# Cross-attention over 16 heads: the heads' outputs moved to their rows by GpSimd, straight through SBUF, instead of by SyncE through DRAM

## The chip, the cores and the metric

One of the cores of a Trainium2 chip runs the program. The metric is device microseconds of one execution of the whole program, median of several executions.

## The reference

Two blocks follow each other on x, 8 batches of 100 rows of 512 values; ctx has 361 rows for each batch. All is float32.

```python
# first block: twice cross-attention with 16 heads of 128, then an MLP of 2048
x = x + cross_attention(layer_norm(x), ctx)      # two layers
x = x + gelu(layer_norm(x) @ w_fc1 + b) @ w_fc2 + b
# second block: cross-attention with 16 heads of 32
x1 = layer_norm(x, ln1_w, ln1_b)
q, k, v = x1 @ q_w + q_b, ctx @ k_w + k_b, ctx @ v_w + v_b      # split into 16 heads of 32
attn = softmax(where(mask, q @ k.T / sqrt(32), min))
out = concat_heads(attn @ v) @ cproj_w + cproj_b
x = x + out
x = x + gelu(layer_norm(x) @ fc_w + fc_b) @ proj_w + proj_b
```

The change touches only what lies between `attn @ v` and `@ cproj_w` in the second block.

## The kernel before

Everything is stored turned: features on the 128 partitions, rows of x on the free axis, in two halves of four batches (`ROWS` = 400 columns). A product in float32 is made of three matmuls of parts: each factor is a high part rounded to the matmul's type and a low part, the rest. ScalarE (ACT) writes the high part, VectorE (DVE) the low one, and GpSimd (POOL) splits weights. The order of every engine is written out by hand, and engines meet only at semaphores. Each engine takes its instructions strictly in order.

**The attention of the second block** is a loop of steps `s`, one for each batch `b` = s // 4 and group of four heads `j` = s % 4 (`NS` = 32 steps, and two more to drain). A step has four units, one head each: turn the probabilities of the unit three back (`turn1`), the scores (`logits1`), a part of the keys of step s + 3 (`keys1`), a third of the weighted sums of values of step s - 2 (`value_sums1`). ACT and DVE do the softmax in between.

**The heads' outputs.** `value_sums1(t)` leaves in a PSUM bank, for group t, a 128 x 400 product whose 128 rows are the features of four heads and whose 400 columns are four probability sets. Only the four diagonal blocks of 32 x 100 are wanted. ACT writes the whole product's high part to `heads_out` (`value_sum1_high`, which the profile shows as a write to qs by line 1234), DVE its low part (`value_sum1_low`, qs by line 1495; it raises `y_lo`). In program order both stand in the fourth unit of step t + 2. There is one buffer `heads_out` alone (`qs[1]`). PE may begin `value_sums1(t + 1)` in the first unit of the next step only when `y_lo` says that the low part of t is written, since both use one PSUM bank.

From `heads_out` the blocks go to `attnT` (the profile's qT), where `project1` reads them: at step 19 (`S_CPROJ`) for the first four batches, after the loop for the rest. A block stays on its 32 partitions and only changes columns. SyncE (SP) does it in two transfers by way of DRAM: `save_heads(t)` writes all of `heads_out` (400 KB) to `y_parts`, line 626; `load_heads(t)` waits for that landing, for `c_mm` if the batch is of the second half (`attnT` is free again only when the first `project1` has read it), and reads the four blocks back, line 636. ACT may write `heads_out` for t when save t - 1 has landed:

```python
            act.wait_ge(S.y_out, 16 * s)
```

**SP's queue** begins all transfers of the program. In step s it stands like this: save heads s - 3, `load_k(s + 1)` (keys of the next step back from DRAM, `k<-k_parts`, line 621), `save_k(s + 2)`, context, mask and queries when due, load heads s - 3, then weights (`load_jobs`, line 558). A weight tile goes to one of three staging buffers, and the load waits until POOL has split the tile three before it (`w_ready`).

**POOL's queue** is a list of weight tiles with due times, `JOBS`, in whose gaps the list `extra` puts other work by due times of its own: the loop step counts from `T_ATT1` = 304. In the loop it splits the tiles of `cproj_w` (in_1c, due at steps 14 and 30) and of the MLP (due at step 20), splits the context of batches 2 to 7 (`second_context`, lines 779 and 781, once in four steps), converts masks, and does parts of layer norms 7 and 8 (`norm_sum`, `norm_square_sum`, `norm_scale`, lines 792 to 813). An extra runs as soon as POOL comes to it and its semaphores allow; the due time sets its place only.

Of the kernel before, what the change touches and what calls it, by code (L numbers as in the profile page):

```python
# [12 lines left out]
F32 = mybir.dt.float32  # L13
# [3 lines left out]
P = 128  # L17
BATCH, LQ, LK, D = 8, 100, 361, 512
NB = BATCH // 2
ROWS = NB * LQ  # L20
LT = LK + 1
DC = D // P
# [4 lines left out]
HG = 4  # L27
HD1 = 32
# [14 lines left out]
NS = 2 * 16  # L43
# [74 lines left out]
T_ATT1 = 304  # L118
# [91 lines left out]
def build(nc, T, out):  # L210
# [5 lines left out]
           ("L1_xattn_fc_b", "L1_xattn_proj_b", ACT.Gelu_apprx_tanh)]  # L216

    k_dram = nc.dram_tensor("k_parts", [NS, P, 2, LT], F32, kind="Internal").ap()
    y_dram = nc.dram_tensor("y_parts", [NS, P, 2, ROWS], F32, kind="Internal").ap()
    q_dram = nc.dram_tensor("q_parts", [BATCH, P, 2, 4, LQ], F32, kind="Internal").ap()  # L220

    with ExitStack() as ctx:
# [60 lines left out]
        attnT, heads_out = qT, qs[1]  # L283
# [13 lines left out]
        def sem(name):  # L297
            return ctx.enter_context(nc.semaphore(name))
# [77 lines left out]
        S.y_hi = sem("y_hi")  # L376
        S.y_lo = sem("y_lo")
        S.at_in = sem("at_in")
        S.y_out = sem("y_out")
        S.k1_out = [sem(f"k1_out{k}") for k in range(2)]  # L380
        S.k3_in = [sem(f"k3_in{k}") for k in range(2)]
        S.k1w_in = sem("k1w_in")
# [23 lines left out]
        def f32(ap):  # L406
            return ap.bitcast(F32)
# [115 lines left out]
        AHEAD, BEHIND = 3, 2  # L523
# [27 lines left out]
        def _(sp):  # L551
# [57 lines left out]
            def save_k(s):  # L609
                sp.wait_ge(S.k1_lo, s + 1)  # L610
                sp.dma_start(k_dram[s], f32(kT[:, s % 2])).then_inc(S.k1_out[s % 2], 16)

            def load_k(s):

                sp.wait_ge(S.k1_out[s % 2], 16 * (s // 2 + 1))
                if s >= 2:
                    sp.wait_ge(S.s1_mm, HG * (s - 2) + HG)
                else:
                    sp.wait_ge(S.o_mm, DC * GN)
                for k, _, k_part in PARTS3:  # L620
                    sp.dma_start(f32(k3[k * HD1:(k + 1) * HD1, s % 2]),
                                 k_dram[s, :, k_part].rearrange("(i r) n -> r i n", i=HG)).then_inc(S.k3_in[s % 2], 16)

            def save_heads(t):
                sp.wait_ge(S.y_lo, t + 1)
                sp.dma_start(y_dram[t], f32(heads_out[:])).then_inc(S.y_out, 16)

            def load_heads(t):

                b, j = divmod(t, 4)  # L630
                sp.wait_ge(S.y_out, 16 * (t + 1))
                if b >= NB:
                    sp.wait_ge(S.c_mm, DC)
                for i in range(HG):
                    r, a = slice(i * HD1, (i + 1) * HD1), j * ROWS + b % NB * LQ
                    sp.dma_start(f32(attnT[r, :, a:a + LQ]), y_dram[t, r, :, i * LQ:(i + 1) * LQ]).then_inc(S.at_in, 16)  # L636

            def load_values_weight():
                sp.wait_ge(S.v_tmp, HG * GN)
                sp.wait_ge(S.up_mm, 3)  # L640
                sp.wait_ge(S.dn_mm, 1)
                for j in range(4):
                    sp.dma_start(w1_raw[:, j, 1, :], T["1v"][j]).then_inc(S.v1w_in, 16)
# [54 lines left out]
            save_k(1)  # L698
            load_k(0)
            for s in range(NS + BEHIND):  # L700
                if s >= BEHIND + 1:
                    save_heads(s - BEHIND - 1)
                if s + 1 < NS:
                    load_k(s + 1)
                if s + AHEAD - 1 < NS:
                    save_k(s + AHEAD - 1)
                if s % 4 == 1 and s // 4 + 2 < BATCH:
                    load_ctxT(4 * GN + s // 4 + 2)
                if s % 4 == 2 and s // 4 + 2 < BATCH:
                    load_mask(s // 4 + 2)  # L710
                if s - 1 - S_Q1 in range(4):
                    save_q(4 + s - 1 - S_Q1)
                if s % 4 == 3 and s // 4 + 1 in range(2, BATCH):
                    load_q(s // 4 + 1)
                if s >= BEHIND + 1:
                    load_heads(s - BEHIND - 1)
                load_jobs(jobs_due(T_ATT1 + s - 1) + STAGE)
            save_heads(NS - 1)
            load_heads(NS - 1)
            for F in range(NF):  # L720
                load_jobs(jobs_due(T_MLP[1] + F - 1) + STAGE)
                if F - FF in range(DC):
# [10 lines left out]
        def _(pool):  # L733
# [73 lines left out]
            def norm_scale(li):  # L807
                k = norm_buffer(li)
                pool.wait_ge(S.ln_rstd, 2 * li + 2)
                for c in range(DC):  # L810
                    y = ln_c[k][:, c, :]
                    pool.wait_ge(S.ln_cs, DC * BY_POOL.index(li) + c + 1)
                    nc.gpsimd.tensor_tensor(y, y, lnb[:, 1, :], ALU.mult).then_inc(S.ln_y, 1)  # L813

            extra = [(due, 3, convert_mask, b) for b, due in enumerate(MASK_DUE)]
            extra += [(T_ATT1 + 4 * (b - 2) + 2.2, 2, second_context, b) for b in range(2, BATCH)]
            for n0, li in LN_GROUP.items():
# [2 lines left out]
            extra += [(s7 + 0.3, 0, norm_sum, 7), (s7 + 2.9, 0, norm_square_sum, 7), (s7 + 6.6, 0, norm_scale, 7),  # L820
                      (s8 + 0.95, 0, norm_sum, 8),
                      (s8 + 4.6, 0, norm_square_sum, 8), (s8 + 8.6, 0, norm_scale, 8)]
            extra.sort(key=lambda e: e[:2])
            done = 0
            for j in range(len(JOBS)):
# [406 lines left out]
        def _(act):  # L1232
# [115 lines left out]
            def value_sum1_high(s):  # L1348
                act.wait_ge(S.a_mm, s + 1)
                if s:  # L1350
                    act.wait_ge(S.y_out, 16 * s)
                else:
                    act.wait_ge(S.qs_out[1], 64)
                high(heads_out[:, 0, :], bank[A1_BANK][:, 0:ROWS], col_c("L1_xattn_v_b", s % 4)).then_inc(S.y_hi, 1)
# [563 lines left out]
```

## Time and profile before

| | us |
|---|---|
| median of three runs | 2254.26 |
| the runs | 2253.84, 2254.26, 2258.37 |
| profiled execution | 2260.57 |
| its span, first to last instruction | 2258.8 |
| PE busy | 2161.1 (96%) |
| DVE busy | 1605.4 (71%) |
| ACT busy | 1183.9 (52%) |
| POOL busy | 943.8 (42%) |
| loop of the second block, about | 1790 to 2105 |

The profiled execution is 6.3 us longer than the median of the others. The views are: the windows (busy time of each engine in a stretch), the timeline of an engine (start, duration, instruction, and in brackets how long the engine was idle before and what ended that), the view of one tile, and the chain of what ended last. Times in the timelines count from the start of the span.

### The profile page before, as it was taken

To read this page: it belongs to the slowest core of one execution; us is meant where nothing else is said; L and a number is where in the kernel's file an instruction comes from. 1 tells how busy PE (TensorE), PEld (TensorE's weight loads), DVE (VectorE), ACT (ScalarE), POOL (GpSimd) and SP (SyncE) were. 2 spreads that over 40 slices of the span, in tenths; PEclk is the share of its full clock that TensorE was granted. 3 is DMA by queue.
4 is the path that set the end of the run, shared out by engine and by line. 5 is a ranking of instruction groups with operands and counts; after the bars stand their busy time and mean duration, and the time that the engine had idled before them with its cause. 6 is when DMAs were issued, how large, how long until landed. Compare 5 with 4: busy or idle time off the path is not lost.

```text
span 2258.8 us, 36858 instructions
## 1 busy us (share of the span) xinstructions
PE 2161.1 (96%) x12468; PEld 2099.6 (93%) x12468; DVE 1605.4 (71%) x3635; ACT 1183.9 (52%) x2838; POOL 943.8 (42%) x898
## 2 busy tenths in 40 slices
PE   6999999999999999999999999999999899998899
PEld 5999999999999999999999999998899778887899
DVE  6777688777778877777887777777466487788353
ACT  4555465555555555555555555565243376667232
POOL 4314444241444424234342424432788332232597
PEclk9999999999999999999999999999999999998999
DMA  4646455554645555464555546454543667765243
GB/s 136 140 87 142 102 121 101 120 128 83 151 101 113 102 125 122 85 148 105 110 110 116 126 83 151 109 102 83 139 125 103 167 189 199 206 199 160 84 132 108
DMA packets 162454, 283.08 MB, mean 125 GB/s; under 512 B 35424, under 2 KB 92896, under 8 KB 162272
## 3 DMA queue, kind: packets, MB, share of 16 engines
q1 hardware_dynamic: 162272, 280.73, 52.5%
q8 instruction: 105, 1.72, 0.3%
q14 instruction: 77, 0.63, 0.1%
HBM read 237.66 MB, written 29.88 MB: 118 GB/s over the span
## 4 chain that ended last, share of the span: by engine, by line
PE 80%; DVE 6%; DMA 4%; ACT 3%; POOL 3%; issue 2%; SPq 2%; POOLq 0%; DVEq 0%; ACTq 0%
PE bank L838 76%; PE bank L926 3%; POOL mring L759 1%; DMA ctxN_raw<-in_ctx 1%; POOL mring L757 1%; DVE ln_c L1548 1%; DVE hT L1495 1%; SPq L636 1%; DVE lnb L1541 1%; PE bank L1106 1%; ACT prob L1340 1%; DMA k<-k_parts 1%; DVE prob L1662 1%; POOL ln_c L813 1%; DMA y_parts<-qs 0%
## 5 line engine op out<-in xcount | busy, mean ns | idle before, releaser
L838 PE MATMUL bank<-ctxT,kring 128*128 128x362 f32 x3456 | 629.6, 330 | 4.4 <-DVE qs L1495 2.7
L757 POOL TENSOR_SCALAR mring<-stage 128x512 fp32r<-128x512 f32 x325 | 233.3, 718 | 899.2 <-PE bank L838 734.2
L838 PEld LDWEIGHTS bank<-ctxT,kring 128*128 128x128 f32 x3456 | 587.2, 190 | 7.6 <-issue 4.7
L838 PE MATMUL bank<-pT,ctxN 128*128 128x400 f32 (+1 forms) x2304 | 470.0, 351 | 0.6 <-DVE U L1499 0.3
L759 POOL TENSOR_TENSOR mring<-stage,mring 128x512 fp32r<-128x512 f32 x325 | 444.9, 1369 | 27.1
L838 PEld LDWEIGHTS bank<-pT,ctxN 128*128 128x128 f32 (+1 forms) x2304 | 407.1, 188 | 2.4 <-issue 1.2
L838 PE MATMUL bank<-hT,mring 128*128 128x400 f32 x1608 | 320.0, 348 | 13.8 <-DVE hT L1495 10.5
L838 PEld LDWEIGHTS bank<-hT,mring 128*128 128x128 f32 x1608 | 296.1, 190 | 18.3 <-issue 15.0
L838 PE MATMUL bank<-U,mring 128*128 128x400 f32 x1536 | 303.3, 348 | 8.1 <-issue 6.3
L838 PEld LDWEIGHTS bank<-U,mring 128*128 128x128 f32 x1536 | 275.3, 188 | 10.3 <-issue 7.9
L1234 ACT ACTIVATE kT<-bank,cols 128x361 fp32r<-128x361 f32 (+1 forms) x288 | 160.8, 558 | 211.8 <-PE bank L838 211.7
L1499 DVE TENSOR_TENSOR ctxN<-ctxN_raw,ctxN 128x384 fp32r<-128x384 f32 x256 | 189.2, 742 | 81.9 <-ACT ctxN L1234 81.9
L1234 ACT ACTIVATE U<-bank 128x400 fp32r<-128x400 f32 x256 | 127.8, 499 | 146.2 <-PE bank L838 144.3
L1499 DVE TENSOR_TENSOR U<-bank,U 128x400 fp32r<-128x400 f32 x256 | 146.2, 571 | 74.8 <-ACT U L1234 73.8
L1577 DVE TENSOR_SCALAR_CACHE_REDUCE prob<-bank 100x362 f32<-100x362 f32 x256 | 135.1, 528 | 88.1 <-PE bank L838 88.0
L1282 ACT ACTIVATE prob<-prob,stat 100x362 f32<-100x362 f32 x256 | 151.1, 590 | 74.7 <-DVE prob L1577 74.7
L1234 ACT ACTIVATE pT<-bank 128x300 fp32r<-128x300 f32 x384 | 160.0, 417 | 54.0 <-PE bank L926 37.6
L1499 DVE TENSOR_TENSOR pT<-bank,pT 128x300 fp32r<-128x300 f32 x384 | 175.6, 457 | 5.8 <-ACT pT L1234 5.8
L1234 ACT ACTIVATE ctxN<-ctxN_raw 128x384 fp32r<-128x384 f32 x256 | 131.7, 516 | 85.3 <-DMA ctxN_raw<-in_ctx 85.2
L838 PE MATMUL bank<-kT,qT 128*100 128x362 f32 x768 | 169.2, 328 | 4.2 <-DVE kT L1495 4.2
L1499 DVE TENSOR_TENSOR part<-gtmp,part 128x400 fp32r<-128x400 f32 x64 | 75.3, 1178 | 136.6 <-ACT part L1234 136.3
L1495 DVE SCALAR_TENSOR_TENSOR kT<-bank,cols,kT 128x361 fp32r<-128x361 f32 (+1 forms) x288 | 168.2, 584 | 4.6 <-ACT kT L1234 4.6
(103 smaller groups left out, 2942.1 us busy)
## 6 DMA issues: line engine op xcount, KB each, us to landing
ctxT_raw<-in_ctx SPq DMA_DIRECT2D x72, 724.0 KB, 7.5
ctxN_raw<-in_ctx SPq DMA_DIRECT2D x256, 192.0 KB, 3.6
k<-k_parts SPq DMA_DIRECT2D x96, 181.0 KB, 3.7
stage<-in_wk SPq DMA_DIRECT2D x64, 256.0 KB, 4.1
stage<-in_wq SPq DMA_DIRECT2D x64, 256.0 KB, 4.5
stage<-in_wv SPq DMA_DIRECT2D x64, 256.0 KB, 4.0
stage<-in_wo SPq DMA_DIRECT2D x64, 256.0 KB, 2.7
stage<-in_fa SPq DMA_DIRECT2D x64, 256.0 KB, 2.6
```

The costliest lines, as they stand in the source:

```text
L636: sp.dma_start(f32(attnT[r, :, a:a + LQ]), y_dram[t, r, :, i * LQ:(i + 1) * LQ]).then_inc(S.at_in, 16)
L757: nc.gpsimd.tensor_scalar(hi, src, 1.0, 1.0, ALU.mult, ALU.mult).then_inc(S.w_hi, 1)
L759: nc.gpsimd.tensor_tensor(lo, src, f32(hi), ALU.subtract).then_inc(S.w_ready, 1)
L813: nc.gpsimd.tensor_tensor(y, y, lnb[:, 1, :], ALU.mult).then_inc(S.ln_y, 1)
L838: mm = pe.matmul(dst, parts_l[a], parts_r[b], start=first and k == 0, stop=last and k == len(order) - 1)
L926: mm = pe.transpose(bank[T_BANK][:, t * LQ:(t + 1) * LQ], prob[0:LQ, n % PB, t * P:(t + 1) * P], ident[0:LQ, 0:LQ])
L1106: mm = pe.transpose(bank[T1_BANK[u % 2]][:, t * LQ:(t + 1) * LQ], prob1[0:LQ, u % PB, t * P:(t + 1) * P], ident[0:LQ, 0:LQ])
L1234: return nc.scalar.activation(dst, src, ACT.Identity, bias=bias)
L1282: nc.scalar.activation(x, x, ACT.Exp, scale=-1.0, bias=nmax[0:LQ, k:k + 1], accum_out=denom[0:LQ, k:k + 1]).then_inc(S.exp_ready, 1)
L1495: return nc.vector.scalar_tensor_tensor(out=dst, in0=src, scalar=bias, in1=f32(hi), op0=ALU.add, op1=ALU.subtract)
L1499: return nc.vector.tensor_tensor(dst, src, f32(hi), ALU.subtract)
L1577: nc.vector.tensor_scalar(prob[0:LQ, k, 0:LT], bank[2 + n % 2][0:LQ, 0:LT], -SCALE0, None, ALU.mult, ALU.min, accum_out=nmax[0:LQ, k:k + 1 ...
```

## The change

`save_heads` and `load_heads` leave SP's queue, and with them the DRAM tensor `y_parts` and the semaphore `y_out`. `move_heads(t)` on POOL waits for `y_lo` (and for `c_mm` from t = 16 on) and begins four transfers, each from one block of `heads_out` to its columns of `attnT`. ACT's write of `heads_out` for t now waits until all four transfers of t - 1 have landed (`at_in`). Each `move_heads(t)` is an extra with due time step t + 2.8. The number of matmuls and of ACT, DVE and POOL compute instructions stays as it was.

```diff
-            def save_heads(t):
-                sp.wait_ge(S.y_lo, t + 1)
-                sp.dma_start(y_dram[t], f32(heads_out[:])).then_inc(S.y_out, 16)
-
-            def load_heads(t):
-
-                b, j = divmod(t, 4)
-                sp.wait_ge(S.y_out, 16 * (t + 1))
-                if b >= NB:
-                    sp.wait_ge(S.c_mm, DC)
-                for i in range(HG):
-                    r, a = slice(i * HD1, (i + 1) * HD1), j * ROWS + b % NB * LQ
-                    sp.dma_start(f32(attnT[r, :, a:a + LQ]), y_dram[t, r, :, i * LQ:(i + 1) * LQ]).then_inc(S.at_in, 16)
...
             for s in range(NS + BEHIND):
-                if s >= BEHIND + 1:
-                    save_heads(s - BEHIND - 1)
...
-                if s >= BEHIND + 1:
-                    load_heads(s - BEHIND - 1)
                 load_jobs(jobs_due(T_ATT1 + s - 1) + STAGE)
-            save_heads(NS - 1)
-            load_heads(NS - 1)
...
+            def move_heads(t):
+
+                b, j = divmod(t, 4)
+                pool.wait_ge(S.y_lo, t + 1)
+                if b >= NB:
+                    pool.wait_ge(S.c_mm, DC)
+                for i in range(HG):
+                    r, a = slice(i * HD1, (i + 1) * HD1), j * ROWS + b % NB * LQ
+                    nc.gpsimd.dma_start(f32(attnT[r, :, a:a + LQ]), f32(heads_out[r, :, i * LQ:(i + 1) * LQ]))\
+                        .then_inc(S.at_in, 16)
+
...
+            extra += [(T_ATT1 + BEHIND + t + 0.8, 1, move_heads, t) for t in range(NS)]
...
-                    act.wait_ge(S.y_out, 16 * s)
+                    act.wait_ge(S.at_in, 64 * s)
```

POOL's queue around steps 13 to 15, before. The splits of the four tiles of in_1c (lines 757 and 759, into mring) are followed by the context split (779, 781):

```order
L757 TENSOR_SCALAR mring<-stage 128x512 [waits q1_mm,w_in1]
L759 TENSOR_TENSOR mring<-stage,mring 128x512 [waits w_hi]
L757 TENSOR_SCALAR mring<-stage 128x512 [waits q1_mm,w_in2]
L759 TENSOR_TENSOR mring<-stage,mring 128x512 [waits w_hi]
L757 TENSOR_SCALAR mring<-stage 128x512 [waits q1_mm,w_in0]
L759 TENSOR_TENSOR mring<-stage,mring 128x512 [waits w_hi]
L779 TENSOR_SCALAR ctxT<-ctxT_raw 128x724 [waits ctxT_in1]
L781 TENSOR_TENSOR ctxT<-ctxT_raw,ctxT 128x724 [waits cT_hi]
```

The same place now (lines 735, 737, 757, 759, 801 are the split of a tile, the split of the context and the move):

```order
L801 DMA qT<-qs_92 32x2x100 [waits y_lo]
L801 DMA qT<-qs_92 32x2x100 x3
L735 TENSOR_SCALAR mring<-stage 128x512 [waits q1_mm,w_in0]
L737 TENSOR_TENSOR mring<-stage,mring 128x512 [waits w_hi]
L735 TENSOR_SCALAR mring<-stage 128x512 [waits q1_mm,w_in1]
L737 TENSOR_TENSOR mring<-stage,mring 128x512 [waits w_hi]
L735 TENSOR_SCALAR mring<-stage 128x512 [waits q1_mm,w_in2]
L737 TENSOR_TENSOR mring<-stage,mring 128x512 [waits w_hi]
L735 TENSOR_SCALAR mring<-stage 128x512 [waits q1_mm,w_in0]
L737 TENSOR_TENSOR mring<-stage,mring 128x512 [waits w_hi]
L757 TENSOR_SCALAR ctxT<-ctxT_raw 128x724 [waits ctxT_in1]
L759 TENSOR_TENSOR ctxT<-ctxT_raw,ctxT 128x724 [waits cT_hi]
```

Move 11 has come ahead of the four splits, and move 12 (two rows further on) stands behind them and behind the context split.

SP's queue at step 19, before:

```order
L605 DMA q_86<-q_parts 32x4x400 [waits s1_mm,qs_out1,qs_out0]
L605 DMA q_86<-q_parts 32x4x400 x2
L636 DMA qT<-y_parts 32x2x100 [waits c_mm,y_out]
L636 DMA qT<-y_parts 32x2x100 x3
L626 DMA y_parts<-qs_92 128x800 [waits y_lo]
L621 DMA k_87<-k_parts 32x4x362 [waits s1_mm,k1_out1]
```

SP's queue at step 19 now:

```order
L603 DMA q_86<-q_parts 32x4x400 [waits s1_mm,qs_out1,qs_out0]
L603 DMA q_86<-q_parts 32x4x400 x2
L619 DMA k_87<-k_parts 32x4x362 [waits s1_mm,k1_out1]
L619 DMA k_87<-k_parts 32x4x362 x2
L609 DMA k_parts<-kT 128x724 [waits k1_lo]
```

The wait for `c_mm` has gone from SP. It stands now on POOL, ahead of a layer norm's sum (line 770) and the splits of the MLP's tiles:

```order
L801 DMA qT<-qs_92 32x2x100 [waits c_mm,y_lo]
L801 DMA qT<-qs_92 32x2x100 x3
L801 DMA qT<-qs_92 32x2x100 [waits c_mm,y_lo]
L801 DMA qT<-qs_92 32x2x100 x3
L770 TENSOR_TENSOR lnb<-xT 128x400 [waits qs_out0,c_add]
L773 TENSOR_TENSOR lnb<-lnb,xT 128x400 [waits ln_sum] x2
L735 TENSOR_SCALAR mring<-stage 128x512 [waits c_mm,w_in1]
```

These are moves 16 and 17; four tile splits follow, and then move 18.

## Rows read from the trace of the kernel before

**Rows 1.** Windows: stretch, length, busy us of PE, PEld, DVE, ACT, POOL; PE clock, DMA share, GB/s.

```profile
1945.90:1949.50 3.60, 3.58 (x15) 3.46 (x16) 2.09 (x6) 1.46 (x4) 0.00 (x0) 0.62 0.83 243
```

**Rows 2.** Timeline of PE: its three longest waits for a transfer in the loop.

```profile
1945.92 0.41 PE L1095 MATMUL bank<-k,q 96*100 96x362 f32 x1 [2.85 <-DMA k<-k_parts]
...
2007.80 0.41 PE L1095 MATMUL bank<-k,q 96*100 96x362 f32 x1 [4.50 <-DMA k<-k_parts]
...
2105.46 11.36 PE L838 MATMUL bank<-qT,w 128*128 128x400 f32 x48 [6.59 <-DMA qT<-y_parts]
```

**Rows 3.** Tile y_parts: issue ns (min/median/max) on SP, and issue to landing.

```profile
L636 SPq DMA_DIRECT2D qT<-y_parts x128: 538/594/974, 1815.4 to 2103.2; - x128
...
DMA to landing us min/median/max: 2.0/3.0/5.3
```

**Rows 4.** One size on two engines: POOL's timeline, and the chain's line for DVE.

```profile
1815.20 1.05 POOL L801 TENSOR_TENSOR lnb<-ln_q 128x400 f32<-128x400 f32 x1 [3.19 <-ACT ln_q L1240]
```

```profile
1813.51 0.57 DVE ln_c L1525
```

**Rows 5.** Timeline of ACT and DVE: the heads of t = 31 written, high and low.

```profile
2096.34 0.60 ACT L1234 ACTIVATE qs<-bank,cols 128x400 fp32r<-128x400 f32 x1 [2.04 <-DMA y_parts<-qs]
```

```profile
2096.97 0.63 DVE L1495 SCALAR_TENSOR_TENSOR qs<-bank,cols,qs 128x400 fp32r<-128x400 f32 x1 [2.06 <-ACT qs L1234]
```

**Rows 6.** Timelines of POOL and PE at steps 7 and 8.

```profile
1851.54 4.29 POOL L813 TENSOR_TENSOR ln_c<-ln_c,lnb 128x400 f32<-128x400 f32 x4 [7.13 <-DVE lnb L1541]
```

```profile
1859.64 0.70 PE L838 MATMUL bank<-pT,v 128*128 128x400 f32 x3
```

**Rows 7.** Timelines of SP, POOL and PE at steps 15 and 16.

```profile
1929.75 2.47 SPq L636 DMA_DIRECT2D qT<-y_parts  x4
1932.27 0.58 SPq L558 DMA_DIRECT2D stage<-in_1c  x1
```

```profile
1936.85 0.62 POOL L757 TENSOR_SCALAR mring<-stage 128x512 fp32r<-128x512 f32 x1 [24.94 <-DMA stage<-in_1c]
...
1938.81 0.90 POOL L779 TENSOR_SCALAR ctxT<-ctxT_raw 128x724 fp32r<-128x724 f32 x1
...
1942.39 1.72 POOL L781 TENSOR_TENSOR ctxT<-ctxT_raw,ctxT 128x724 fp32r<-128x724 f32 x1
```

```profile
1935.96 0.70 PE L838 MATMUL bank<-pT,v 128*128 128x400 f32 x3
```

**Rows 8.** Timelines of SP, POOL and PE at steps 19 to 22.

```profile
1980.16 2.46 SPq L636 DMA_DIRECT2D qT<-y_parts  x4
```

```profile
1981.96 2.18 POOL L795 TENSOR_TENSOR lnb<-lnb,xT 128x400 f32<-128x400 f32 x2
```

```profile
1981.35 0.70 PE L838 MATMUL bank<-pT,v 128*128 128x400 f32 x3
...
1996.06 0.71 PE L838 MATMUL bank<-pT,v 128*128 128x400 f32 x3
```

**Rows 9.** Timelines of POOL and PE at steps 24 to 29.

```profile
2019.23 2.24 POOL L805 TENSOR_TENSOR lnb<-lnb,ln_q 128x400 f32<-128x400 f32 x2 [8.81 <-ACT ln_q L1240]
...
2055.09 4.30 POOL L813 TENSOR_TENSOR ln_c<-ln_c,lnb 128x400 f32<-128x400 f32 x4 [32.57 <-DVE lnb L1541]
```

```profile
2026.86 0.70 PE L838 MATMUL bank<-pT,v 128*128 128x400 f32 x3
...
2062.35 0.71 PE L838 MATMUL bank<-pT,v 128*128 128x400 f32 x3
```

**Rows 10.** Timelines of DVE and ACT: heads of t = 27 written, t = 28 begun.

```profile
2069.04 0.63 DVE L1495 SCALAR_TENSOR_TENSOR qs<-bank,cols,qs 128x400 fp32r<-128x400 f32 x1 [0.83 <-ACT qs L1234]
```

```profile
2075.91 0.57 ACT L1234 ACTIVATE qs<-bank,cols 128x400 fp32r<-128x400 f32 x1
```

**Rows 11.** Timeline of DVE: one multiplication, without and with POOL at work.

```profile
1925.71 0.41 DVE L1676 TENSOR_SCALAR prob<-prob,stat 100x361 f32<-100x361 f32 x1
...
1989.49 1.05 DVE L1676 TENSOR_SCALAR prob<-prob,stat 100x361 f32<-100x361 f32 x1
```

More of the change, by code:

```diff
@@ L218, in build @@
     k_dram = nc.dram_tensor("k_parts", [NS, P, 2, LT], F32, kind="Internal").ap()
-    y_dram = nc.dram_tensor("y_parts", [NS, P, 2, ROWS], F32, kind="Internal").ap()
     q_dram = nc.dram_tensor("q_parts", [BATCH, P, 2, 4, LQ], F32, kind="Internal").ap()
@@ L378, in build @@
         S.at_in = sem("at_in")
-        S.y_out = sem("y_out")
         S.k1_out = [sem(f"k1_out{k}") for k in range(2)]
```

## The prediction

> **What bounds the kernel now.** I read four views, in this order. The table of engines says PE: busy 96% of the span; DVE follows with 71%. So a change pays only where PE waits, and costs wherever it makes PE wait. The change acts only in the loop of the second block, so I went to PE's timeline there and looked for idle time that a transfer ended. There are three such places [rows 2]: 2.85 and 4.50 us for keys that SP had begun to load late, and 6.59 us ahead of the last projection, for the last heads to come back from DRAM. These are what the change can win. Then I listed who waits for a transfer of heads today: ACT, before it writes the single buffer heads_out. Last came POOL's timeline, for everything that will now stand in one queue with the moves. The trace holds no transfer that POOL begins, so the price of one must be bounded.
>
> **What is removed.** SP loses five issues a step, four of them 0.594 us each [rows 3], so over 2.4 us of a step of about 9 (34 steps in some 315 us), and its wait for c_mm. This is off PE's path except through the late keys. The DRAM traffic goes too, and nothing else waits for that. The most it gives is the 2.85 and 4.50 of rows 2 and a part of the tail.
>
> **What a move costs.** From the wait's release to the landing of the last block: three further issues c and one issue-to-landing l, d = 3c + l. For c the low end is SP's 0.594 for the same shape [rows 3], the high end POOL's longest instruction here, 1.72 [rows 7]. I take 1.1: on a 128 x 400 addition or subtraction POOL needs 1.05 where DVE needs 0.57 [rows 4], a factor 1.85, and 0.594 x 1.85 = 1.1. It is an estimate. For l the view gives 2.0 to 5.3, median 3.0 [rows 3]; I take 3.0, and 2.0 as the low end because DRAM is left out. So d = 6.3, between 3.8 and 8.2. The Trainium skill (DMA: Bandwidth & Descriptors, "Anatomy of one DMA — SWDGE (gpsimd) path") gives a fixed 2.0 us and bytes/436e3 for a transfer that GpSimd begins, 2.06 us for these 25,600 bytes; with it in place of 3.0, d would be 5.4, inside my range, and the sum below some 10 us smaller. No row shows it.
>
> **Where the wait lands.** Before, heads_out was free once one save had landed. Now it needs POOL to have come to the move, and d. When it is late, ACT stops at its write, with the turned probabilities and exponentials of the next heads queued behind it; DVE stops at the low part; PE stops at value_sums1 of the next group (bank<-pT,v), in the next step's first unit. ACT's and DVE's writes take 0.60 and 0.63 with 0.03 between [rows 5], so with the hand-over PE goes on 1.3 us after the landing. With P the time at which POOL reaches a move, PE loses P + d + 1.3 minus the time at which that matmul stood before: P + 7.6 minus it. Where moves follow freely, P is the end of DVE's write. The narrowest gap to ACT's next write is from 2069.67 to 2075.91, 6.2 us [rows 10], against d = 6.3: just enough. So the cost lies where POOL is held. I keep before's clock at each place, since an earlier loss moves both sides alike.
>
> a) norm_scale of layer norm 7 stands ahead of move 4 and cannot start before 1851.54; it ends at 1855.83. 1855.83 + 7.6 - 1859.64 = 3.8 [rows 6].
>
> b) Move 12 stands behind four splits of in_1c and a context split. The fourth tile is issued by SP only at the end of step 15, at 1932.27, and POOL starts to split it 4.58 later; the split takes 1.96, the context 5.3 [rows 7]. Before, nothing on POOL minded those 24.94 us of waiting. SP's relief brings the issue forward by the four loads ahead, 2.5, to 1929.8. Move 12 then begins at 1929.8 + 4.58 + 1.96 + 5.3 = 1941.6; 1941.6 + 7.6 - 1935.96 = 13.3. It swallows the 2.85 of rows 2, so 10.5 net.
>
> c) Move 16 waits for c_mm, the last matmul of project1(0), as SP did until 1980.16; but SP's wait held no buffer, since the save had been made. Now ACT cannot write group 17. 1980.16 + 7.6 - 1981.35 = 6.4 [rows 8].
>
> d) Move 18 stands behind the sum of norm 8 (1.05 + 2.18, say 3.3) and four splits. Move 17 begins at 1987.8 (after c), its issues end at 1992.2, sum 1995.5, three splits 2001.4. The fourth tile is loaded after the first split, 1997.5 + 4.6 = 2002.1, split 2004.0, plus 7.6 = 2011.6. PE would be there at 1996.06 + 6.4 = 2002.5. That is 9.1; less the 4.50 of rows 2, 4.6 [rows 7, 8].
>
> e) norm_square_sum ahead of move 21 ends at 2021.47: + 7.6 - 2026.86 = 2.2. f) norm_scale 8 ahead of move 25 ends at 2059.39: + 7.6 - 2062.35 = 4.6 [rows 9].
>
> g) The tail. Move 27 begins at 2069.7, its issues end at 2074.1, the first of four splits at 2076.1; the fourth tile lands 4.6 later, split 2082.6. Moves 28, 29 and 30 then follow with 7.6 each, since little other work is left between, to 2105.4, and move 31 lands 6.3 later, 2111.7, against 2105.46: 6.2. The 6.59 of rows 2 is not won: SP's way took one short landing for each group and the long way only once, now each group takes the whole d.
>
> Sum: 3.8 + 10.5 + 6.4 + 4.6 + 2.2 + 4.6 + 6.2 = 38.3. After the wait of 2.85 the granted clock was 0.62 over 3.6 us [rows 1], which is 1.4 us lost; three new waits of that kind (a, c, f) add 4.2. Together 42.5. The profiled execution of 2260.57 (span 2258.8) would become about 2303; it lies 6.3 above the median of the runs, and on that median I put the difference: 2254.3 + 42.5 = 2297.
>
> **Low and high ends.** With d = 3.8 (c = 0.6) the same working gives 1.3 + 7.9 + 3.9 + 0.1 + 0 + 2.1 - 5.8 = 9.5, so 2264. With d = 8.2 (c = 1.72): 5.7 + 12.3 + 8.3 + 9.1 + 4.1 + 6.5 + 16.4 = 62, plus 4 of clock, plus about 10 because some ten groups have gaps like the 6.2 of rows 10 and each then loses about one: 76, so 2330.
>
> **Rivals.**
> 1. *The relief of SP wins.* If moves are cheap and the held places b to d mostly vanish in the lead that ACT and DVE have over PE, what stays is the gain: 2.85 + 4.50 + 5.8 of the tail = 13, so 2241. For it: SP's lateness is real. Against it: PE's next value sum stands behind y_lo by the program, and at c no lead helps, since the landing itself starts after c_mm. It decides only if d is below about 2.5, where the sum crosses zero; the shortest landing alone is 2.0. Chance 0.04.
> 2. *Cheap moves, small loss.* d near 4 to 5: places b and c stay, the tail repays a part. 2264 to 2280, middle 2272. Chance 0.24.
> 3. *The move itself bounds every step.* d of 8 and more, so that each group is late and not only the held ones: 2330 at 8.2, and each further microsecond some 20 more. For it: GpSimd is the slow engine in rows 4. Chance 0.18.
> 4. *VectorE holds up the descriptors.* DVE's multiplication of 361 numbers takes 0.41 alone and 1.05 while POOL worked [rows 11], so the two do shut each other out. If each of four issues waits for one such multiplication, d grows by 4 x 0.41 = 1.6 to 7.9; with about 9 us of sum for each microsecond of d, 2297 + 15 + 10 for the narrow gaps = 2322. The Trainium skill (SBUF — State Buffer, "SBUF: two separate sides") says that a DMA begun by GpSimd cannot write its descriptors while VectorE runs an operation that takes both port pairs; the 1.05 of rows 11 agrees that the pair is shared, but no row shows a transfer held by it. Chance 0.1.
> 5. *The change does not do what it says*: another store or load of heads stays on SP. In the order nothing of the kind is left. Chance 0.01; its time is 2254.
>
> **How the numbers follow.** My forecast, d = 5.5 to 7.5 and the held places as worked out, has 0.43: 2297, its own range 2285 to 2315. Rivals 2, 3, 4 have 0.24, 0.18, 0.1, rivals 1 and 5 0.05. The range for 8 in 10 leaves out rival 1, the lowest part of 2 and the upper half of 3: 2266 to 2332. About 0.2% of the time, 4.5 us, is what a measurement of this kernel tells from no change. Slower than that: 0.92 (forecast, 3, 4 and nearly all of 2). Within: 0.04. Faster: 0.04.
>
> **What would show each step.** In the changed kernel's timeline POOL's DMA rows give c at once, the tile view l. ACT rows qs of line 1224 should carry waits for a transfer qT<-qs, the longest near step 15 (about 15 us) and at steps 19 and 21, short ones at 7, 27 and from 31 on, and none or nearly none at steps such as 10 to 13. PE's waits for k<-k_parts should be gone. If waits stand at every step, rival 3 or 4 is right; if the wait at step 15 is below 5 us, POOL's order does not bind as I read it, and the forecast is wrong from b on.

## The result, and the profile after

| | before | changed |
|---|---|---|
| median, us | 2255.42 | 2283.22 |
| lowest and highest of 4 runs each | 2253.84, 2258.37 | 2281.08, 2283.95 |
| profiled execution, its span | 2260.57, 2258.8 | 2283.91, 2281.8 |
| PE busy | 2161.1 | 2168.4 |
| mean granted clock over the loop | 0.94 | 0.90 |

The ratio is 1.012, 95% interval 1.0103 to 1.0138: the change costs 27.8 us. The forecast was 42.5 more, so the direction and most of the places were right, and the loss came to two thirds of it.

Nearly all of it lies in the loop. From the loop's first wait for keys to the last projection, before took 1793.04 to 2105.46 = 312.4 us; the changed kernel takes 1791.52 to 2129.63 = 338.1, that is 25.7 more. (The two spans differ by 23.0 only, because the profiled execution of before was itself one of its longer ones.) Here is PE's timeline of the changed kernel: every wait of the loop's value sums, and the last projection. It answers to [rows 2] and to the matmuls of [rows 6 to 9].

```profile
1791.52 0.62 PE L1085 MATMUL bank<-k,q 96*100 96x362 f32 x1 [4.05 <-DMA k<-k_parts]
...
1863.28 0.78 PE L828 MATMUL bank<-pT,v 128*128 128x400 f32 x3 [4.00 <-DVE qs L1485]
1881.20 0.77 PE L828 MATMUL bank<-pT,v 128*128 128x400 f32 x3 [0.35 <-DVE qs L1485]
1948.25 1.34 PE L828 MATMUL bank<-pT,v 128*128 128x400 f32 x3 [10.13 <-DVE qs L1485]
1966.42 0.79 PE L828 MATMUL bank<-pT,v 128*128 128x400 f32 x3 [1.15 <-DVE qs L1485]
1996.07 1.34 PE L828 MATMUL bank<-pT,v 128*128 128x400 f32 x3 [4.08 <-DVE qs L1485]
2022.07 1.34 PE L828 MATMUL bank<-pT,v 128*128 128x400 f32 x3 [8.48 <-DVE qs L1485]
2051.33 0.78 PE L828 MATMUL bank<-pT,v 128*128 128x400 f32 x3 [1.33 <-DVE qs L1485]
2091.11 1.34 PE L828 MATMUL bank<-pT,v 128*128 128x400 f32 x3 [4.58 <-DVE qs L1485]
2098.61 0.78 PE L828 MATMUL bank<-pT,v 128*128 128x400 f32 x3 [0.59 <-DVE qs L1485]
2106.42 1.34 PE L828 MATMUL bank<-pT,v 128*128 128x400 f32 x3 [0.18 <-DVE qs L1485]
2115.22 1.34 PE L828 MATMUL bank<-pT,v 128*128 128x400 f32 x3 [0.48 <-DVE qs L1485]
2129.63 5.53 PE L828 MATMUL bank<-qT,w 128*128 128x400 f32 x29 [1.33 <-DMA qT<-qs]
```

The waits of 2.85 and 4.50 for keys in [rows 2] are gone, and so is most of the 6.59. In their place stand 36.7 us of waits for heads. The kernel before had four short waits for heads too, all in its last steps. PE's timeline of before:

```profile
2069.82 1.34 PE L838 MATMUL bank<-pT,v 128*128 128x400 f32 x3 [0.59 <-DVE qs L1495]
2077.30 1.34 PE L838 MATMUL bank<-pT,v 128*128 128x400 f32 x3 [0.51 <-DVE qs L1495]
2084.78 1.34 PE L838 MATMUL bank<-pT,v 128*128 128x400 f32 x3 [0.48 <-DVE qs L1495]
2092.64 1.87 PE L838 MATMUL bank<-pT,v 128*128 128x400 f32 x9 [0.76 <-DVE qs L1495]
```

The difference, 36.7 - 13.9 - 2.3 = 20.4 unrounded, is four fifths of the loop's loss. The windows cut the same loss in another way: line for line they show the stretch (the loop as measured above), its length, busy time of PE, PEld, DVE, ACT and POOL, clock, DMA share and GB/s, first of before and then of the changed kernel.

```profile
1793.04:2105.46 312.42, 273.98 (x1540) 241.92 (x1541) 238.72 (x720) 205.05 (x538) 82.28 (x81) 0.94 0.67 186
```

```profile
1791.52:2129.63 338.11, 282.59 (x1541) 248.51 (x1541) 237.61 (x720) 204.67 (x537) 148.64 (x207) 0.90 0.48 132
```

PE's busy time rose by 8.6 us for as many matmuls, at a mean clock of 0.90 in place of 0.94, and its idle time by 17.1. So 3.3 of the 20.4 us of new waits came out of small gaps that PE had anyway, and the slower matmuls added 8.6. Over the 3.6 us behind each of the four waits of 10.13, 4.08, 8.48 and 4.58 the granted clock was 0.50, behind that of 4.00 it was 0.67. (In the second row POOL's busy time also counts its transfers.)

**Who releases the waits.** The sums of ACT's waits for the landing and of PE's for the heads (us, times, longest), from the table of waits of the changed kernel, and the tile view of the moves: first POOL's issue time, then the time to landing.

```profile
ACT qs L1224 <- DMA qT<-qs: 45.5, 9, 12.0
...
PE bank L828 <- DVE qs L1485: 35.3, 11, 10.1
```

```profile
L801 POOL DMA_DIRECT2D qT<-qs x128: 536/536/752, 1813.2 to 2127.8; - x128
...
DMA to landing us min/median/max: 1.7/2.3/6.2
```

An issue costs POOL 0.54 us, half of the 1.1 of the prediction and even less than SP's 0.594 of [rows 3]. The median landing is 2.3, not 3.0. But the landing depends on company. POOL's timeline at three places, with the landings of the four transfers of each move behind it:

```profile
1851.69 4.29 POOL L791 TENSOR_TENSOR ln_c<-ln_c,lnb 128x400 f32<-128x400 f32 x4 [2.98 <-DVE lnb L1531]
...
1855.93 2.19 POOL L801 DMA_DIRECT2D qT<-qs  x4
```

```profile
DMA to landing us min/median/max: 1.8/3.6/4.2
```

```profile
1936.33 0.62 POOL L735 TENSOR_SCALAR mring<-stage 128x512 fp32r<-128x512 f32 x1 [7.50 <-DMA stage<-in_1c]
...
1943.37 2.19 POOL L801 DMA_DIRECT2D qT<-qs  x4
```

```profile
DMA to landing us min/median/max: 1.7/1.7/1.8
```

```profile
2012.46 0.63 POOL L735 TENSOR_SCALAR mring<-stage 128x512 fp32r<-128x512 f32 x1 [4.76 <-DMA stage<-in_fa]
...
2014.38 2.19 POOL L801 DMA_DIRECT2D qT<-qs  x4
```

```profile
DMA to landing us min/median/max: 3.3/3.8/4.5
```

At the first and third place SP begins its keys 0.5 to 0.6 us after the move, and the landings take up to 4.2 and 4.5 us. SP's timeline beside the first:

```profile
1856.54 1.26 SPq L619 DMA_DIRECT2D k<-k_parts  x3
1857.85 0.43 SPq L609 DMA_DIRECT2D k_parts<-kT  x1
```

At the second SP's last key transfer began 3.2 us before the move and the next came 12.8 after it, and all four land in 1.7 to 1.8. The longest landing of all, 6.2, belongs to the move at 1910.30, beside keys and 724 KB of context that SP began within 1.4 us of it. That company is the cause is read from these places; no run varies it alone. From a move's start to PE going on it is 7.35 (1855.93 to 1863.28) and 7.69 (2014.38 to 2022.07) in company, and 4.88 alone (1943.37 to 1948.25, 1991.19 to 1996.07). The prediction had 7.6 everywhere: its flat value fits the places in company, by too dear an issue and too cheap a last landing, and is 2.7 too long where a move is alone.

### The profile page after: what moved, and what is told of

Read it like the earlier page. It is cut to its first block, busy times and chain, and to the rows that moved or that the text cites. A ratio compares the mean times of both kernels' runs of the same rounds, so it can differ in the third digit from the quotient of the medians.

```text
span 2281.8 us, 36826 instructions
## 1 busy us (share of the span) xinstructions
PE 2168.4 (95%) x12468; PEld 2103.6 (92%) x12468; DVE 1603.2 (70%) x3635; ACT 1183.2 (52%) x2838; POOL 1015.1 (44%) x1026
## 4 chain that ended last, share of the span: by engine, by line
PE 77%; POOL 8%; DMA 5%; DVE 4%; ACT 3%; issue 3%; SPq 1%; POOLq 0%; DVEq 0%; ACTq 0%
PE bank L828 72%; POOL mring L737 4%; PE bank L916 3%; POOL mring L735 2%; DMA qT<-qs 2%; DMA ctxN_raw<-in_ctx 1%; PE bank L1096 1%; POOL qT L801 1%; POOL ln_c L791 1%; ACT prob L1330 1%; DVE qs L1485 1%; DVE prob L1652 1%; ACT qs L1224 0%; DMA stage<-in_fb 0%; PE bank L1085 0%
```

## The experiments

All of them begin from the changed kernel unless it is said otherwise. Each ratio is to the kernel before, timed on the same chip. The runs stand on different chips, on which the kernel before had medians of 2254.84 to 2259.03, so a difference of a few us between two medians is less sure than that of their ratios.

| | what | median, us | ratio, 95% interval |
|---|---|---|---|
| changed | moves by POOL | 2283.22 | 1.012, 1.0103 to 1.0138 |
| e1 | the same transfers begun by SP | 2256.23 | 1.0003, 0.9991 to 1.0015 |
| e2 | SP saves to DRAM, POOL loads back | 2250.02 | 0.9977, 0.9964 to 0.9989 |
| e3 | weight tiles spread on POOL | 2264.4 | 1.004, 1.0025 to 1.0054 |
| e4 | eight transfers a move | 2309.52 | 1.0241, 1.0225 to 1.0256 |
| e5 | no transfer at all | 2260.05 | 1.0, 0.9988 to 1.0012 |
| e6 | moves 0.3 of a step earlier in POOL's list | 2280.41 | 1.0093, 1.0077 to 1.011 |
| e8 | groups 16 and 17 by DRAM | 2278.59 | 1.009, 1.0072 to 1.0107 |
| e7 | e3 + e6 + e8 | 2258.78 | 1.0002, 0.9988 to 1.0016 |
| e10 | e6 with gaps in norm_scale | 2272.78 | 1.0064, 1.0046 to 1.0082 |
| e11 | e7 with gaps in norm_scale | 2246.69 | 0.9956, 0.9939 to 0.9972 |
| e9 | e2 + e3's places | 2246.32 | 0.9939, 0.9923 to 0.9954 |
| e12 | before + e3's places | 2246.13 | 0.9968, 0.9955 to 0.998 |

The theory was: what costs is a held buffer, that is ACT waiting to write heads_out while POOL stands at other work; it is neither the issue's price nor the direct way. The first rival was the price of a move at every step; the second, that the direct way itself is bad.

### e1 and e2: which part of the change costs

e1 keeps the direct way through SBUF and gives the four issues back to SP, at the place of the old `load_heads`:

```diff
+                sp.wait_ge(S.y_lo, t + 1)
+                if b >= NB:
+                    sp.wait_ge(S.c_mm, DC)
...
+                    sp.dma_start(f32(attnT[r, :, a:a + LQ]), f32(heads_out[r, :, i * LQ:(i + 1) * LQ])).then_inc(S.at_in, 16)
```

> The direct route of the change, but SyncE begins the four transfers of each group, at the place in its queue where it loaded the heads before; ACT waits for their landing as in the changed kernel. Theory (the time is lost where GpSimd's other work or the wait for c_mm stands ahead of a move, and heads_out stays held): the waits of ACT near steps 7, 27 and the long one at step 15 go, the one after c_mm stays with about 4 us of PE, SyncE's own weight loads near steps 16 and 22 hold some moves; about 2258, between before and a few us more. Rival 1 (the issuer: transfers begun by GpSimd are slow as such): every move gets shorter, 2250 or less. Rival 2 (the route: holding the one buffer for a whole move costs everywhere, whoever begins it): as the changed kernel, 2278 to 2285.

Measured: 2256.23, no difference from before. PE still stands 3.94 us behind c_mm, for which SP now waits while the buffer is held, and its waits for heads come to 8.7 us in all, against 2.3 before; those for DVE's turned probabilities are 16.1 against 12.7. Against that the waits of 2.85 and 4.50 for keys are gone, and the last one is 2.70 in place of 6.59. So with SP as the issuer the gains and the losses of the direct way cancel, and the loss of the change comes with POOL as the issuer, by what stands in its queue.

e2 does the opposite: SP saves heads_out to DRAM as before and ACT waits for that save; only the loads back are POOL's.

```diff
-                pool.wait_ge(S.y_lo, t + 1)
+                pool.wait_ge(S.y_out, 16 * (t + 1))
...
-                    act.wait_ge(S.at_in, 64 * s)
+                    act.wait_ge(S.y_out, 16 * s)
```

> SyncE saves the heads to DRAM as before and ACT waits for that alone; GpSimd loads the four blocks back, at the place of the changed kernel's moves and with its wait for c_mm. Theory: GpSimd may be as late as it likes, since nobody but the projection waits for it; ACT's waits at steps 7, 15, 19, 21, 27 are gone, and PE's two waits for late keys (2.85 and 4.50) are gone too as SyncE has four issues less in a step: 2243 to 2250, faster than before. Rival 1 (GpSimd's transfers as such cost, by the shared port or the DMA engines): 2270 or more. Rival 2 (the lateness of SyncE is unchanged by four issues less): 2255.

Measured: 2250.02, faster than before by 0.23%. From e2's table of waits:

```profile
POOL qT L810 <- DMA y_parts<-qs: 114.3, 21, 12.9
ACT qs L1233 <- DMA y_parts<-qs: 2.1, 1, 2.1
PE bank L837 <- DVE qs L1494: 1.3, 3, 0.6
```

POOL is as late as in the changed kernel, at the same places, and begins the same 128 transfers. But its lateness holds no buffer: PE's waits for heads fall from 35.3 to 1.3. So the price is the buffer's release on a queue that stands elsewhere, not POOL's issues (0.533 each here). What e2 can't tell apart is the source, DRAM here and SBUF in the changed kernel; e1 had the SBUF source without the loss.

### e3, e8, e6: the held places one by one

e3 spreads the weight tiles that stood four in a row, over steps 13 to 16, 21 to 24 and 28 to 31, so that moves come between them. Terms b and d should go.

```diff
-        add(T_ATT1 + 14, "1c", 0, j)
-        add(T_ATT1 + 30, "1c", 1, j)
+        add(T_ATT1 + 13 + j, "1c", 0, j)
+        add(T_ATT1 + 28 + j, "1c", 1, j)
...
-        add(T_ATT1 + 20, *t)
+        add(T_ATT1 + 21 + k, *t)
```

> The changed kernel, with the twelve tiles that GpSimd splits in the loop spread over steps (one a step, at 13 to 16, 21 to 24, 28 to 31) instead of four at a time, so that a move stands between each two and none stands behind the tile that has yet to be loaded. Theory: PE's waits of 10.1 us (step 16) and 8.5 us (step 22) shrink to 0 to 3 each, those at steps 8, 20 and 29 stay; 2264 to 2270. Rival 1 (issuer or route costs everywhere): within 3 us of the changed kernel, 2280 to 2286. Rival 2 (the waits are only moved to other steps): 2275 to 2283.

Measured: 2264.4, 18.8 less than the changed kernel. The waits of 10.13 and 8.48 are gone from PE's timeline; those of places a, c and f stay at 3.79, 4.07 and 4.89.

e8 takes away only POOL's wait for c_mm while a buffer is held: SP saves groups 16 and 17 to DRAM, ACT waits for the save alone.

```diff
+                if s in (19, 20):
+                    save_heads(s - 3)
...
-                pool.wait_ge(S.y_lo, t + 1)
+                if t in (16, 17):
+                    pool.wait_ge(S.y_out, 16 * (t - 15))
```

> The changed kernel, but groups 16 and 17, the two whose rows are free only after c_mm, go by way of DRAM: SP saves them, POOL loads the blocks back, and ACT waits for the save alone. It isolates term c. Theory: the wait of PE of 4.08 us at 1996.07 goes, and about 1.4 of clock with it; the other waits stay: from 2283.2 to 2276 to 2279. Rival: the save on SP's queue and the slower loads make move 18 later by as much, and the time stays at 2281 to 2284.

Measured: 2278.59, 4.6 less (4.8 by the loops of the two traces). The wait of 4.08 is gone, the one behind it is 8.73 as against 8.48. Term c is real and has its own price.

e6 puts each move 0.3 of a step earlier in POOL's list, so that moves 4, 21 and 25 come ahead of the norm's instructions instead of behind them (terms a, e and f).

```diff
-            extra += [(T_ATT1 + BEHIND + t + 0.8, 1, move_heads, t) for t in range(NS)]
+            extra += [(T_ATT1 + BEHIND + t + 0.5, 1, move_heads, t) for t in range(NS)]
```

> The changed kernel with one number altered: the moves' due times are 0.3 of a step earlier, which puts moves 4, 21 and 25 ahead of the layer norms' instructions that they stood behind, and nothing else in another order. Theory: PE's waits of 4.0, 1.3 and 4.6 us at steps 8, 25 and 29 go, with about 1.4 us of slow clock after each of the two long ones: 2283 - 13 = 2270 to 2274. Rival (the moves there were slow to land because of key transfers, not held by GpSimd's order): at most 4 us gained, 2279 to 2283.

Measured: 2280.41. That is a miss: the gain is 2.8 by the medians, 3.5 by the loops of the two traces (334.6 against 338.1), some 6 by the ratios, where 9 to 13 were expected. ACT's waits at steps 7 and 27 had gone as planned, yet PE stood at almost the same places for almost as long, only now for DVE. PE's timeline of e6:

```profile
1854.19 0.73 PE L1096 MATMUL bank<-ident,prob 100*128 100x100 f32 x3 [3.12 <-DVE pT L1489]
```

```profile
2080.85 0.73 PE L1096 MATMUL bank<-ident,prob 100*128 100x100 f32 x3 [3.96 <-DVE pT L1489]
```

POOL's and DVE's timelines of e6 say why. Look at the multiplication of 361 numbers (line 1666), 0.41 us in [rows 11] when DVE is alone:

```profile
2073.98 2.12 POOL L801 DMA_DIRECT2D qT<-qs  x4 [6.92 <-DVE qs L1485]
2076.11 4.00 POOL L791 TENSOR_TENSOR ln_c<-ln_c,lnb 128x400 f32<-128x400 f32 x4
```

```profile
2075.80 0.47 DVE L1652 CUSTOM_DVE_ANT_0 prob<-bank,mask_off 100x361 f32<-100x361 f32 x1
...
2076.40 3.92 DVE L1666 TENSOR_SCALAR prob<-prob,stat 100x361 f32<-100x361 f32 x1
2080.24 0.46 DVE L1489 TENSOR_TENSOR pT<-bank,pT 128x300 fp32r<-128x300 f32 x1
```

It begins 0.3 us after norm_scale's first multiplication and ends 0.2 after its fourth; at step 7 it takes 4.03 us. In the changed kernel the same four POOL instructions stand beside the same DVE work, but there POOL reaches them early and waits for DVE's reciprocal to release the first, and DVE's timeline has this instead:

```profile
1852.12 0.83 DVE L1666 TENSOR_SCALAR prob<-prob,stat 100x361 f32<-100x361 f32 x1
```

### e10 and e11: is it the gapless run?

The new theory: four POOL instructions that all stand ready behind the move leave DVE no chance in between; with a wait between them they do. The rival was that the move's own descriptors shut DVE out. e10 is e6 with each multiplication made to wait for the one before it, the same work at the same place (the half step in the expectation is e6's 0.3):

```diff
                     pool.wait_ge(S.ln_cs, DC * BY_POOL.index(li) + c + 1)
+                    if c and li in (7, 8):
+                        pool.wait_ge(S.ln_y, DC * li + c)
                     nc.gpsimd.tensor_tensor(y, y, lnb[:, 1, :], ALU.mult).then_inc(S.ln_y, 1)
```

> The kernel of e6 (moves due half a step earlier) with one further edit: each of the four multiplications of norm_scale 7 and 8 on POOL waits for its predecessor's ln_y, as the three additions of a norm sum already do. Same work at the same place, only that the four no longer stand without a gap. Theory: in e6 the multiplication of DVE that came just behind POOL's first one took 4.03 and 3.92 us in place of 0.41, since POOL had all four ready behind the move and never let the shared port go; with a gap DVE gets in behind the first, takes 0.8 to 1.4, and PE's waits of 3.12 and 3.96 shrink to below 1 each. That is 5 to 6.5, and about 2 of clock: from 2280.4 to 2271 to 2275. Rival: DVE is shut out by something else at these places (the move's own descriptors), then its multiplication stays at 3 to 4 us and the time at 2279 to 2282.

Measured: 2272.78, 7.6 less than e6. POOL's timeline and DVE's of e10 at step 7:

```profile
1846.64 2.18 POOL L803 DMA_DIRECT2D qT<-qs  x4 [2.17 <-DVE qs L1487]
1848.84 4.64 POOL L793 TENSOR_TENSOR ln_c<-ln_c,lnb 128x400 f32<-128x400 f32 x4
```

```profile
1849.05 1.06 DVE L1668 TENSOR_SCALAR prob<-prob,stat 100x361 f32<-100x361 f32 x1
1851.64 0.84 DVE L1668 TENSOR_SCALAR prob<-prob,stat 100x361 f32<-100x361 f32 x1
```

The four take 4.64 in place of 4.02, DVE's multiplication 1.06 in place of 4.03, and PE's waits of 3.12 and 3.96 are gone (at step 27 one of 1.00 is left). The move still stands directly ahead, so the descriptors are not the cause. The Trainium skill (SBUF — State Buffer, "SBUF: two separate sides") says that the port pair which VectorE and GpSimd share is an exclusive lock held for one instruction, by whichever starts first. The 1.06 agrees with that. The 3.92 and 4.03 do not: there VectorE was out for four instructions.

A run without a gap is not enough to do that. In the changed kernel the first of the four waits for the reciprocal, but nothing holds the other three, as ACT had scaled all their inputs 27 us before. ACT's timeline of the changed kernel:

```profile
1822.64 2.18 ACT L1237 ACTIVATE ln_c<-ln_c,cols 128x400 f32<-128x400 f32 x4
```

Yet DVE came in behind the first and took 0.83, and at step 7 of before, e2, e3, e8, e9 and e12, where POOL also stands idle until the reciprocal, it took 0.82 or 0.83. Only behind a move, with no wait of POOL ahead of the first, was it shut out (4.03 in e6, 4.02 in e7). So the gap is shown to be a cure; why the run behind a move differs from the one behind a wait is not shown.

e11 is e7, all places mended at once, with the same gaps. e7 first:

> All held places mended at once in the changed kernel: tiles spread over steps, moves ahead of the norms, and groups 16 and 17 alone go through DRAM (SyncE saves, GpSimd loads after c_mm), so that ACT need not wait for c_mm. Theory: what stays is the changed kernel without its losses and with SyncE's relief: 2264 (tiles spread alone) - 13 - 5 = 2246 to 2251, faster than before. Rival (a further loss of the route that no held place explains, 1 us or less in each of 30 groups): 2258 or more.

Measured: 2258.78, the rival's number; PE stood 3.03 and 3.96 us for the same DVE multiplications as in e6 (4.02 and 3.93 us long).

> The kernel of e7 (tiles spread, moves earlier, groups 16 and 17 through DRAM) with the same gap in norm_scale 7 and 8. e7 was missed because PE waited 3.03 and 3.96 us there. Theory: both go down to below 1, 5 to 6 us and some clock: from 2258.8 to 2250 to 2254, so that moves begun by GpSimd beat the kernel before by little. Rival (the losses only move on, to the moves behind these places): 2256 to 2259.

Measured: 2246.69, 12.1 below e7 and 0.44% faster than before. That is 3.3 us below the theory's range, but 2.1 of it is the chip, on which the kernel before was faster by as much (2256.89 against 2259.03); by the traces' loops e11 is 10.8 shorter than e7. PE's waits for DVE's turned probabilities fell by 6.2 (18.8 to 12.6); the rest of the 10.8 I can't place.

### e4: what a microsecond of a move is worth

e4 makes eight transfers of a move, the high and the low part apart.

> The changed kernel, with each move made of eight transfers (high and low part apart) instead of four: four more issues of about 0.6 us, so that a move is 2.4 us longer and the bytes are the same. Theory: each of the seven held places, and the three further groups of the tail, lose 2.4 more, 24 us, and steps with narrow gaps a few: 2305 to 2315. Rival (a held place costs what stands ahead of the move, its own length hardly counts, or ACT's lead hides it): 2284 to 2292.

Measured: 2309.52. POOL's issues take 0.496 each, the last begins 7 x 0.496 = 3.5 us after the first in place of 1.65, so a move is 1.8 longer; the kernel lost 26.3, some 14 us for each microsecond. The prediction's working had nine, and ten more over the last 1.9 for the narrow gaps, which is about the same. That the time fell into the expected range is partly luck: the expectation had a move 2.4 longer at ten us of loss for each, and it was 1.8 at fourteen. It also shows how little room the single buffer leaves.

### e5: no transfer at all

ACT and DVE write the four diagonal blocks of 32 x 100 themselves, straight to their columns of attnT (groups 16 and 17 through corners of heads_out and one POOL copy after c_mm).

```diff
+                for i in range(HG):
+                    r = slice(i * HD1, (i + 1) * HD1)
+                    high(head_block(s, i, 0), bank[A1_BANK][r, i * LQ:(i + 1) * LQ],
+                         col_c("L1_xattn_v_b", s % 4)[r]).then_inc(S.y_hi, 1)
```

> No transfer at all: ACT and DVE write only the four diagonal blocks, 32 partitions by 100 columns each, straight into attnT (four small instructions each in place of one of 400 columns); the groups 16 and 17, for which attnT is not yet free, go to two corners of heads_out, and GpSimd copies them after c_mm in one instruction each. Theory (the transfers are the whole loss and the whole of SyncE's lateness): no wait of ACT for a transfer, no 6.6 us wait ahead of the last projection, keys in time but for SyncE's weight chain; against it some 0.6 us more on ACT and on DVE in each step ahead of y_lo, hidden by PE in most steps: 2238 to 2250. Rival (the longer ACT and DVE writes bound the steps, since the score-to-turn chain has only two units of lead): 2255 to 2270.

Measured: 2260.05, ratio 1.0: the rival held. From e5's groups by shape (count, busy, mean ns):

```profile
L1232 ACT ACTIVATE qT<-bank,cols 32x100 fp32r<-32x100 f32 x120 | 39.9, 333 | 3.4 <-PE bank L834 1.1
L1496 DVE SCALAR_TENSOR_TENSOR qT<-bank,cols,qT 32x100 fp32r<-32x100 f32 x120 | 38.1, 318 | 6.3 <-ACT qT L1232 1.2
```

A sixteenth of the elements takes about half of the time of the whole (0.60 and 0.63 in [rows 5]), so the four cost 1.33 and 1.27 us a step. PE's waits for DVE's turned probabilities rose to 24.4 us from 12.7 before, which ate the transfers' saving.

### e9 and e12: what is worth keeping

e9 is e2 with e3's places.

> SyncE saves and GpSimd loads the heads for all groups, and GpSimd's tiles are spread over steps as well. Theory: PE's remaining waits for keys (1.21 and 3.59 us) come from SyncE standing at a weight load until GpSimd has split a tile, and go: 2250 - 5 - 1.4 = 2243 to 2246. Rival (they come from the transfers' own landing time): 2249 to 2251.

Measured: 2246.32, ratio 0.9939 (0.9923 to 0.9954), at the upper end of the theory's range; both waits for keys are gone from PE's timeline. e12 is the control: the kernel before, with e3's places and nothing else.

> The kernel before, with the spread tiles of e3 alone: SP keeps both ways through DRAM, no instruction is added or taken away. It is the control for e9 and e11: how much of their gain belongs to the tiles' places and how much to the route. Theory: before, no wait of POOL held the heads, so the places bring only what SP's bunched weight loads cost, the waits of PE of 2.85 and 4.50 for late keys; with five issues of heads a step still on SP the keys stay partly late. 2250 to 2255, and the gains of e9 and e11 then belong to the route. Rival: the bunched tiles alone were the cause of both waits, and the control gives what e9 gives, 2245 to 2248, so that the route adds nothing.

Measured: 2246.13, ratio 0.9968 (0.9955 to 0.998). The theory written ahead of it had the route as the cause of e9's gain, and is mostly wrong. PE's timeline of e12: the last projection, and no other transfer to wait for in the loop but the first keys.

```profile
1789.08 0.41 PE L1095 MATMUL bank<-k,q 96*100 96x362 f32 x1 [3.81 <-DMA k<-k_parts]
...
2090.53 10.35 PE L838 MATMUL bank<-qT,w 128*128 128x400 f32 x48 [5.80 <-DMA qT<-y_parts]
```

The loop takes 301.4 us against 312.4: the waits for keys in [rows 2] went by spreading the tiles alone, with all of SP's issues in place. e9's loop takes 296.5 (1792.48 to 2088.96) and its last wait 3.46. By the ratios e9 is 0.3% better than e12, with intervals that only just keep apart, on different chips; by the medians they are equal. So the route through POOL gives between nothing and some 0.3%. A version as fast by the medians costs no new code: other due times for twelve tiles.

## Why the forecast was right, and where it was not

**a, 3.8 forecast, 4.00 measured; f, 4.6 and 4.58.** The mechanism was right: a move behind norm_scale, which waits for DVE. The size was right by two errors that cancel, issues of 0.54 in place of 1.1 and last landings of 4.2 and 3.8 in place of 3.0, beside the keys. e6 and e10 add what the prediction did not see: to put the move ahead of norm_scale only helps if DVE is let in.

**b, 13.3 gross, 10.13 measured.** SP's issue of the fourth tile came at 1930.61 (forecast 1929.8), the move at 1943.37 (1941.6). The failed term is d: 4.88 from the move to PE in place of 7.6, as nothing else was in flight. The 2.85 of rows 2 was swallowed, as worked out. e3 confirms the place.

**c, 6.4 forecast, 4.08 measured; e8 confirms it.** The same 2.7 in d, of which 0.4 came back, as c_mm came later against PE (0.80 us before PE's place in place of 1.19).

**d, 9.1 gross, 8.48; e, 2.2 and 1.33.** Right; d was in company.

**g, +6.2 forecast, -6.3 measured.** This is the largest miss, 12.5 of the 17.9 us by which the waits were overestimated (38.3 against 20.4). In the last steps the key transfers run out, and the landings of moves 30 and 31 are all 1.7. POOL's timeline of the changed kernel:

```profile
2109.09 2.19 POOL L801 DMA_DIRECT2D qT<-qs  x4
2115.37 2.27 POOL L801 DMA_DIRECT2D qT<-qs  x4 [4.09 <-DVE qs L1485]
2121.24 2.12 POOL L801 DMA_DIRECT2D qT<-qs  x4 [3.61 <-DVE qs L1485]
2126.20 2.12 POOL L801 DMA_DIRECT2D qT<-qs  x4 [2.84 <-DVE qs L1485]
```

The forecast let each follow after 7.6; they follow after 6.3, 5.9 and 5.0, and PE stands 0.18, 0.48 and at the end 1.33. With the 0.59 ahead of them that is 2.6 against 8.9 of before, its 6.59 and the four short waits of 2.3. The term is d again: the working of g with the d of 3.6 of a lone move would give about -6.8, an estimate from the same rows. Yet the chain of landings that it assumes was not there: ACT's write for move 30 waited 0.63 for PE, and only that for move 31 waited for a landing, 1.15.

**The clock, 4.2 forecast.** Beside the waits the loop lost 25.7 - 20.4 = 5.3, so the sum was near, partly by luck. Its parts were not: the busy time rose by 8.6, as there are five new waits of 4 us and more where three were counted, with a clock of 0.50 behind four of them where 0.62 was taken, and small gaps took back 3.3.

**The step that failed** is thus one: the value taken for d. For c the prediction scaled SP's issue by POOL's slowness in arithmetic, though an issue does no arithmetic; SP's own 0.594 was the nearest row. For l it took one median for all places, where the trace of before already spread from 2.0 to 5.3. d was 3.6 where a move was alone and 6.1 to 6.4 in company (the 4.88, 7.35 and 7.69 less 1.3), so rival 2 (d of 4 to 5) lay between the two kinds of place, and the time, 2283, lies just above its 2264 to 2280 and just below the forecast's own 2285 to 2315. Rival 4, VectorE holding up the issues, did not show: the longest of 128 issues is 0.752. The Trainium skill (SBUF — State Buffer, "SBUF: two separate sides") says that they can be held; no run here shows one held for long. The 2.06 estimated in the prediction from the Trainium skill (DMA: Bandwidth & Descriptors, "Anatomy of one DMA — SWDGE (gpsimd) path") lies between the 1.7 alone and the median of 2.3, and was the better value for l where a move is alone, at b and c; at a, d and f the longest landings of 4.2, 4.5 and 3.8 were above that and above 3.0.

## What to carry to other kernels

Ask of a moved transfer first which buffer its landing frees, and what stands ahead of it in the new queue: in e2 POOL begins as many transfers, as late, but SP's save frees the buffer, and it is 33 us faster. Bound its landing by company, alone and beside the large transfers of the same step, not by one median. And when a version wins, run its side edits alone on the old kernel: here the spread tiles alone took nearly all of what looked like the new route's gain.

## What was not expected of the hardware

- A DMA issue of GpSimd for a 25 KB block within SBUF took 0.536 us (median of 128), SyncE's for the same block from DRAM 0.594, within SBUF 0.597 (e1). For half the block it was still 0.496.
- Such a transfer landed in 1.7 us alone, in up to 4.5 beside key transfers of 181 and 362 KB, and in up to 6.2 with 724 KB of context beside them as well.
- Four GpSimd multiplications of 128 x 400 that stood ready in a row behind its DMA issues kept VectorE's 0.41 us multiplication out for 3.92 and 4.03 us. With a semaphore between them it was 1.06, and they took 4.64 instead of 4.02. Where the first of the four waited for its input and the others did not, it was 0.83. What makes the difference is not shown.
